# Summing four token tiles on TensorE and storing them from ScalarE's queue, and moving two ScalarE copies ahead of an activation-table load

## The reference

```
x = x + xattn(layernorm(x), ctx)            # 4 heads of 64, context of 192 features
xn = layernorm(x)
scores = softmax(xn @ gw + gb)              # 32 experts in 8 groups
# keep the 4 best groups, then the 4 best experts of them; cw = their scores
y = sum over experts e of cw[:, e] * ((silu(xn @ w1[e] + b1[e]) * (xn @ w3[e] + b3[e])) @ w2[e] + b2[e])
z = (silu(xn @ sw1 + sb1) * (xn @ sw3 + sb3)) @ sw2 + sb2      # the shared expert
x = x + y + z
```

## Time and profile before

| | |
|---|---|
| median of 3 runs | 362.8 us (358.01 to 363.51) |
| the profiled execution's own time | 360.53 us |
| its span, first to last instruction | 358.8 us |
| outside the span | 1.73 us |
| mean granted TensorE clock | 0.957 of full speed |
| busy share of the span | PE 88%, DVE 71%, ACT 54%, POOL 50% |

### The profile page before, as it was taken

The page is one execution under the profiler, slowest core; times in us unless marked ns, Lnnn a source line. Parts: engine busy times, 40 slices in busy tenths (PEclk is TensorE's granted clock), DMA queues, the critical chain, the costliest instruction groups (busy, mean ns, idle before and its releaser), DMA issues.

```text
span 358.8 us, 9631 instructions
## 1 busy us (share of the span) xinstructions
PE 314.1 (88%) x2240; PEld 265.0 (74%) x2241; DVE 255.0 (71%) x865; ACT 194.1 (54%) x632; POOL 179.8 (50%) x221
## 2 busy tenths in 40 slices
PE   2998999999999999799999999999999999996000
PEld 1785887978788787478877888998989898985000
DVE  5489777878787785964795666776676676764775
ACT  2386777878777576327312565665656565653000
POOL 4620402656555575715562065666666576656500
PEclk9999999999999999699999999999999999999655
DMA  6899265585822236402424355656666565658798
GB/s 175 264 395 377 82 202 178 221 287 185 311 74 91 76 127 241 172 18 76 143 93 124 99 171 170 194 175 195 184 192 185 167 212 171 191 179 306 272 412 301
DMA packets 33782, 68.96 MB, mean 192 GB/s; under 512 B 5339, under 2 KB 26108, under 8 KB 32092
## 3 DMA queue, kind: packets, MB, share of 16 engines
q1 hardware_dynamic: 26364, 46.95, 40.6%
q0 software_dynamic: 6960, 21.11, 15.9%
q10 hardware_dynamic: 432, 0.59, 0.6%
HBM read 39.87 MB, written 28.77 MB: 191 GB/s over the span
## 4 chain that ended last, share of the span: by engine, by line
PE 76%; DMA 9%; DVE 5%; issue 3%; ACT 2%; SPq 2%; ACTq 1%; POOL 0%; POOLq 0%; DVEq 0%
PE psS L1235 11%; PE psF L103 7%; PE psF L1244 5%; PE psS L1224 5%; PE psF L1235 5%; DMA xn2T_all<-dispatch 4%; PE psS L103 4%; PE psS L985 4%; PE psF L1020 4%; PE psS L993 4%; PE psF L1034 3%; PE psF L939 3%; PE psF L1127 3%; PE psS L1093 3%; DMA w<-shares 2%
## 5 line engine op out<-in xcount | busy, mean ns | idle before, releaser
L677 POOL DMA_INDIRECT shares<-xn2T_all,e_number x81 | 86.2, 1064 | 60.1 <-issue 25.5
L626 POOL DMA_INDIRECT dispatch<-work,slot_now x64 | 64.7, 1010 | 59.2 <-issue 22.2
L1235 PE MATMUL psS<-work,arena 128*128 128x128 f32 x432 | 57.1, 275 | 0.0
L1235 PEld LDWEIGHTS psS<-work,arena 128*128 128x128 f32 x432 | 52.6, 192 | 0.1
L904 ACT ACTIVATE work<-psS 128x256 f32<-128x256 f32 x81 | 30.9, 383 | 17.8 <-PE psS L1224 14.7
L1670 DVE SCALAR_TENSOR_TENSOR work<-psS,b,work 128x128 f32<-128x128 f32 x54 | 18.9, 351 | 27.6 <-ACT work L915 27.3
L1673 DVE COPY arena<-w 128x512 f32 x81 | 35.1, 434 | 2.5 <-issue 2.5
L1224 PE MATMUL psS<-ident,xn2T_all 128*128 128x128 f32 x162 | 31.6, 278 | 3.3 <-DMA xn2T_all<-dispatch 2.2
L1244 PE MATMUL psF<-w,work 128*128 x108 | 32.5, 382 | 0.5 <-DVE work L1670 0.5
L915 ACT ACTIVATE work<-psS,b 128x128 f32<-128x128 f32 x54 | 19.8, 367 | 24.1 <-PE psS L1235 23.1
L1224 PEld LDWEIGHTS psS<-ident,xn2T_all 128*128 128x128 f32 x162 | 21.3, 141 | 15.0 <-DMA xn2T_all<-dispatch 3.9
(11 more groups left out here) (233 smaller groups left out, 778.4 us busy)
## 6 DMA issues: line engine op xcount, KB each, us to landing
xn2T_all<-dispatch SPq DMA_DIRECT2D x81, 160.0 KB, 2.3
w<-in_w SPq DMA_DIRECT2D x6, 1536.0 KB
w<-shares SPq DMA_DIRECT2D x6, 1024.0 KB, 7.7
dispatch<-padding SPq DMA_DIRECT2D x8, 640.0 KB, 9.7
w<-in_w SPq DMA_DIRECT2D x1, 2304.0 KB
w<-shares SPq DMA_DIRECT2D x3, 512.0 KB, 7.0
out<-x SPq DMA_DIRECT2D x3, 512.0 KB, 3.4
hs_ctx<-in_ctxT SPq DMA_DIRECT2D x7, 192.0 KB, 3.2
```

The costliest lines, as they stand in the source:

```text
L626: pool.indirect_dma_start(dispatch, bass.IndirectOffsetOnAxis(ap=slot_now[:, par, n:n + 1], axis=0), xn2[:, par, n // TOPK, :], None).then ...
L677: pool.indirect_dma_start(shares, bass.IndirectOffsetOnAxis(ap=e_number[:, u:u + 1], axis=0), e_y[:, u, :], None).then_inc(added[u], 16)
L1235: ins = pe.matmul(hidden_bank(u)[:, m * P:(m + 1) * P], e_w13k[:, u % UNROLL, k, m * INTER:(m + 1) * INTER], e_xT[:, u % 3, k, :], start=( ...
```

## The change

First, at the end: PE puts the first group (tiles 0 to 3) of `x` and of the four planes through the identity matrix and adds them up in two PSUM banks, ACT copies the sum back into `x` and issues its store from its own DMA queue. DVE leaves these four tiles out of its three first-half adds and no longer does the first of the six last adds; SP no longer issues the first store, and waits for one event fewer ahead of the others. Second, in ACT's last attention step: `weights_out(0)` and `weights_now(1)` stand before `silu(1, 1)` and the three `round_chunk`, no longer behind them.

```
@@ scalar, step, not front
+                    weights_out(0)
+                    weights_now(1)
                     silu(1, 1)
                     for c in range(WHOLE, 6):
                         round_chunk(c)
@@ scalar, the chunks
-                if c != 2:
+                if c not in (0, 2):
                     weights_out(c)
-                if c + 1 < BATCHES:
+                if 1 <= c and c + 1 < BATCHES:
                     weights_now(c + 1)
@@ scalar, at the end
+            act.wait_ge(s["first_psum"], 1)
+            act.activation(x[:, 0:GROUPED[0], :].rearrange("p t d -> p (t d)"), psS[:, 0:GROUPED[0] // 2, :].rearrange("p a n -> p (a n)"),
+                           ACT.Copy).then_inc(s["first_summed"], 1)
+            act.wait_ge(s["first_summed"], 1)
+            act.dma_start(out.rearrange("(t p) d -> p t d", p=P)[:, 0:GROUPED[0], :], x[:, 0:GROUPED[0], :]).then_inc(s["out_done"], 16)
@@ tensor, at the end
+            def first_group(rows, start, stop):
+                for n in range(GROUPED[0] // 2):
+                    ins = pe.matmul(psS[:, n, :], ident[:, :], rows[:, 2 * n:2 * n + 2, :].rearrange("p t d -> p (t d)"), start=start, stop=stop)
+                return ins
+            first_group(x, True, False)
+            for k in range(TOPK - 1):
+                pe.wait_ge(plane_in[k][0], 16)
+                first_group(y_all[:, k], False, False)
+            pe.wait_ge(shares_in[0], 16)
+            first_group(y_all[:, TOPK - 1], False, True).then_inc(s["first_psum"], 1)
@@ vector, at the end
-                    xt = x[:, h * HALF:(h + 1) * HALF, :]
+                    t0 = h * HALF if h else GROUPED[0]
+                    xt = x[:, t0:(h + 1) * HALF, :]
...
-                dve.wait_ge(shares_in[g], 16)
-                dve.tensor_tensor(xt, y_all[:, TOPK - 1, t:t + n, :], xt, ALU.add).then_inc(s["y_summed"], 1)
+                if g >= 1:
+                    dve.wait_ge(shares_in[g], 16)
+                    dve.tensor_tensor(xt, y_all[:, TOPK - 1, t:t + n, :], xt, ALU.add).then_inc(s["y_summed"], 1)
@@ sync, the stores
-                sp.wait_ge(s["y_summed"], g + 1)
-                sp.dma_start(ov[:, t:t + n, :], x[:, t:t + n, :]).then_inc(s["out_done"], 16)
+                if g >= 1:
+                    sp.wait_ge(s["y_summed"], g)
+                    sp.dma_start(ov[:, t:t + n, :], x[:, t:t + n, :]).then_inc(s["out_done"], 16)
```

More of the change, by code:

```diff
@@ L393, in build @@
             ew_ready exT_psum exT_ready eh_psum eg_ready em_ready ey_psum
-            meta_copied shares_landed y_summed out_done""".split()
+            meta_copied shares_landed y_summed first_psum first_summed out_done""".split()
         s = {n: sem(n) for n in names}
@@ L1690, in _ @@
                         st.need(f"plane{k - 1} {h}")
-                    st.did(dve.tensor_tensor(xt, y_all[:, k, h * HALF:(h + 1) * HALF, :], xt, ALU.add), f"plane{k} {h}")
+                    st.did(dve.tensor_tensor(xt, y_all[:, k, t0:(h + 1) * HALF, :], xt, ALU.add), f"plane{k} {h}")
             st.need(f"plane{TOPK - 2} {HALVES - 1}")
```

## The result

| | before | after |
|---|---|---|
| median of 4 runs | 360.4 us (356.37 to 363.51) | 361.81 us (360.11 to 362.85) |
| the profiled execution | 360.53 us | 361.27 us |
| its span | 358.8 us | 359.5 us |
| mean granted clock | 0.957 | 0.959 |

The ratio is 1.0118 with a 95% interval of 1.0064 to 1.0171: within 2%, and slower. The ratio compares the executions of each kernel that lie within 1.5% of its fastest; the kernel before spreads over 2%, so that its slow executions drop out, and the plain medians differ by 0.4%. The time lies 0.7 us from it, inside the range.

A forecast was written before the change was run, and what follows sets the result against it. PE's wait for `cwT` with half clock behind it bounds the middle, first store start and store rate the end. 360.53 us + 0.3 (middle) + 0.3 (end) = 361.1 us; range 356.8 to 364.4.

The forecast's parts named there:

- the new wait on ACT: Last attention step: ACT, free at 143.06, waits 0.4 us for the transposes before the moved `weights_out(0)`.
- PE held at chunk 1 by L1512: PE reaches chunk 1 5.9 us earlier but waits 2.7 us for DVE's L1512, ending at 154.0; 3.15 us gained.
- DVE's L1275 held up by POOL: Last attention step: DVE's 128x2 operation takes 4.08 us beside POOL's three remainders, and neither changes.
- no gain from a second queue: End stores: ACT's own queue adds nothing, the DMA share being already 1.01; best case 0.9 us less, put into the range.
- PE's four-tile sums: Kernel end: each source's sum on PE takes 3.46 us at half clock, 1.73 at full clock.
- I take the fall, +0.3: Middle: clock falls again behind the new hole, costing 3.43 us against 3.15 gained, net +0.3; chance of 361.1 us 0.47.
- both kernels may show either case: Middle: by the Trainium skill's rule, the clock may fall or not in runs of either kernel; no size given.
- rival A: Middle: the new hole leaves the clock up, net -3.15 us, total 357.7 us; chance 0.30.
- give the sum as it stands: Total kept at 361.1 us from the 360.53 execution, though the median shown was 362.8; spread put into the range.
- The term of the tail, +0.3: Kernel end: DVE's first add waits for group 1's share until 349.8, so the first store leaves 0.3 us later.
- Rival B: Kernel end: group 1 lands at 350.8, first store 1.2 us later, total 362.0 us; chance 0.13.
- Rival C: Middle: the early copy does not reach PE, the moved copies gain zero, total 360.8 us; chance 0.05.

The follow-up runs named there:

- the sixth run: Only the two ACT copies moved, plus POOL's three remainders waiting for DVE's `shared_hidden(1)`, against the kernel before: 354.86 us against 360.42, ratio 0.9908.
- the last run: The changed kernel, unaltered, timed a third time against the kernel before: 362.06 us against 359.76, ratio 1.0082.
- the second: Only the four tiles at the end go through PE, ACT copies left in place, against the kernel before: 359.89 us against 360.65, ratio 1.0012.
- the seventh run: Only the four tiles through PE, with group 1's last-plane load issued ahead of group 0's, against the kernel before: 358.13 us against 360.42, ratio 1.0001.
- the third: Kernel before with DVE's `shared_hidden(1)` put in front of norm2(7)'s reciprocal square root, against the kernel before: 357.2 us against 360.65, ratio 0.995.
- the first: Only the two ACT copies moved, the end as before, against the kernel before: 361.35 us against 360.65, ratio 1.0066.
- the ninth run: The changed kernel again, unaltered, against the kernel before, in the batch some 24 us slower: 385.21 us against 384.38, ratio 1.0002.

## Why the prediction was wrong, and where it was right

The steps that were seen as forecast: the new wait on ACT (0.4 us forecast, 0.42 measured); `cwT` in time and `shared_up(2)` at full clock; PE held at chunk 1 by L1512 at an unmoved moment, 3.15 us earlier than before (3.14: 14.13 us after the transposes before, 10.99 after), in a hole of 2.42 us for the 2.7 forecast; DVE's L1275 held up by POOL (4.08 us again, and shown by the sixth run); the clock falling again; the first add of the end waiting for group 1, the stores at 340 GB/s, ACT's store near 353 (352.75), and no gain from a second queue. PE's four-tile sums were forecast at 3.5 us each at half clock; the first two ran at full clock in 1.88 us each, the third took 3.78.

The step that failed is "I take the fall, +0.3", together with the sentence behind it, "both kernels may show either case". It has an error of kind and one of size.

The error of kind decides the sign. The sum was set against one profiled execution that had the fall, and the fall was then charged to both kernels alike. The kernel before escapes it in 15 of 81 executions and then takes 355.4 to 358 us; the changed one was not seen to in 16, nor the copies alone in 12. So rival A was drawn on the wrong kernel: the -3.15 us of an execution without a fall belonged to the kernel before. Among executions with a fall the forecast of about nothing holds for the copies alone, 361.35 us against 361.26; for the whole change the last run has 362.06 against 360.44, and what makes up these 1.6 us is not shown. With it goes the choice to "give the sum as it stands": the profiled execution was 2.3 us below the median on record, and a small loss added to it came out as a forecast below that median.

The error of size: the text took the slow stretch of one trace, 6.87 us, as the price of a fall. In the changed kernel's trace it was 10.2 us, of which 9.5 met work: 4.7 us instead of 3.4, so that the middle came out at +1.30 and not +0.3. That is a matter of the trace and not of the new hole. Of the eight traces with a fall in this place, five have some 6.8 us and three 10.2, and both lengths stand behind the old hole (6.8 before, in the second and the seventh run, 10.2 in the third) and behind the new one (6.8 in the first and the ninth run, 10.2 in the first profile of the changed kernel and in the last run). That the profiled pair differs by 0.7 us, near the 0.6 forecast, is luck: it holds a long stretch against a short one, and 0.78 and 0.51 us gained in code that is the same.

Why the new hole never left the clock up is open. The prediction noted that it stands behind small products. That these make the difference, at the same length of 2.4 us, is argued and was not tested; the trace with a hole of 1.64 us alone and no fall, beside the one with 1.71 and then 1.15 us and a fall, fits it and does not prove it.

The term of the tail, +0.3: its mechanism, the wait in front of the first add, is in all five traces with the new end and the loads in their old order (0.30, 0.34, 0.42, 0.52 and 0.66 us). That the time grows by it is not shown, as the ratios of the second and the seventh run are 1.0012 and 1.0001. Rival B named the right place with too high a price, 1.2 us. Rival C fell. The range held the time, but its upper end, 364.4, does not follow from its own terms: B and 3 us are 365.0.

## What to carry to other kernels

When a wait of an engine is removed, run its order forward to the next event of another engine, and look at what that event waits for: here the next one was held by a third engine's work, and `shared_hidden(1)` moved up on VectorE turned +0.7 us into -5.7 us (354.94 against 360.65). If a price hangs on the clock, ask in how many executions each kernel pays it; one profiled execution can't tell, the times and mean granted clocks of all of them can. Where stores fill the DMA engines, as here with 8.0 us from the first store to the end in most traces, taking adds off an engine gained nothing, as the first store did not leave earlier.

## What was not expected of the hardware

The slow stretches of the clock have one of two lengths in the same place, 6.8 or 10.2 us, also between kernels with the same hole. A hole of 2.4 us is followed by a fall in most executions of one kernel and in all seen of another. Twelve unused products in such a hole, with the copies moved, gave 3.9 us against the kernel before, more than the hole's own length. One batch ran all kernels 24 us slower at much the same granted clock (0.957 to 0.962 in its profiled executions).
